# A decoder layer in split fp32: cross-attention queries made for four batches at a time, P.V for four heads, self-attention queries turned one step earlier

## The reference, cut to what matters

```python
hidden_states = jnp.concatenate([context, latents], axis=1)      # 256 keys a batch
q = (latents @ Wq).reshape(b, q_len, 4, 8, 128)                  # 4 groups of 8 heads
k = (hidden_states @ Wk).reshape(b, kv_len, 4, 128)
v = (hidden_states @ Wv).reshape(b, kv_len, 4, 128)
scores = jnp.einsum('bqhgd,bkhd->bhgqk', q, k) * scale
attn = jax.nn.softmax(scores, axis=-1)
out = jnp.einsum('bhgqk,bkhd->bqhgd', attn, v).reshape(b, q_len, 32 * 128)
x = x + out @ Wo
```

## Time and profile before

| what | value |
|---|---|
| runs | 1053.47 us median of 3 (1052.87 to 1053.89) |
| profiled execution | 1053.37 us, its span 1051.7 us |
| PE matmul | 1027.2 us busy (98%), 6808 matmuls |
| PE weight load | 916.8 us (87%) |
| VectorE, ScalarE, GpSimd | 645.4 (61%), 544.2 (52%), 385.5 us (37%) |
| TensorE's granted clock | 0.998 on average |
| data moved by DMA | 68.5 MB, 65 GB/s |
| self-attention, four groups, feed-forward (starts) | about 39, 317 and 917 us |

### The profile page before, as it was taken

How to read it: one execution, slowest core, us unless ns; L and a number is a source line. 1 busy time by engine, 2 the same in 40 slices (tenths; PEclk the granted TensorE clock), 3 DMA queues, 4 the chain that set the end, 5 groups by cost and what they waited for, 6 DMA issues and landing times.

```text
span 1051.7 us, 18418 instructions
## 1 busy us (share of the span) xinstructions
PE 1027.2 (98%) x6808; PEld 916.8 (87%) x6808; DVE 645.4 (61%) x1369; ACT 544.2 (52%) x1657; POOL 385.5 (37%) x370
## 2 busy tenths in 40 slices
PE   6999999999999999999999999999999999999997
PEld 5677777777889999999999999999999999799996
DVE  6788888887436555546545556555555575556554
ACT  5666666666526555536445446455545456522111
POOL 3544544544235324316224325225234236511110
PEclk9999999999999999999999999999999999999999
DMA  8300111105652003112022111121211013200000
GB/s 327 115 28 21 34 41 42 41 21 141 175 162 82 25 31 112 61 41 61 21 79 63 63 45 55 50 61 51 81 51 51 31 61 122 74 7 20 20 21 21
DMA packets 70114, 68.53 MB, mean 65 GB/s; under 512 B 3984, under 2 KB 53904, under 8 KB 70032
## 3 DMA queue, kind: packets, MB, share of 16 engines
q1 hardware_dynamic: 70032, 67.43, 20.5%
HBM read 48.55 MB, written 18.87 MB: 64 GB/s over the span
## 4 chain that ended last, share of the span: by engine, by line
PE 92%; DVE 4%; ACT 2%; issue 1%; DMA 1%; SPq 0%; POOLq 0%; POOL 0%; DVEq 0%; ACTq 0%
PE bank L218 27%; PE bank L220 26%; PE bank L219 26%; PE bank L945 5%; PE bank L729 2%; PE bank L689 1%; PE bank L693 1%; PE bank L699 1%; ACT Pb L1192 1%; DVE b_nb L1545 1%; PE bank L696 1%; DVE b_max L1542 1%; PE bank L611 1%; DMA rawKV<-in_L_attn_Wv_dram 1%; DVE PTal L1304 0%
## 5 line engine op out<-in xcount | busy, mean ns | idle before, releaser
L548 POOL TENSOR_TENSOR Pb<-Pb,b_rec 128x512 f32<-128x512 f32 x128 | 133.1, 1040 | 353.1 <-DVE b_rec L1549 352.7
L218 PE MATMUL bank<-XTh,WQh 128*128 128x256 f32 x512 | 145.9, 285 | 2.5 <-DVE Ql L1304 2.4
L220 PE MATMUL bank<-XTh,WQl 128*128 128x256 f32 x512 | 144.9, 283 | 0.0
L219 PE MATMUL bank<-XTl,WQh 128*128 128x256 f32 x512 | 144.8, 283 | 0.0
L1192 ACT ACTIVATE Pb<-bank,b_nb 128x256 f32<-128x256 f32 x256 | 119.0, 470 | 40.8 <-DVE b_nb L1545 40.1
L1304 DVE TENSOR_TENSOR Ol<-bank,Oh 128x256 fp32r<-128x256 f32 x128 | 54.0, 422 | 116.0 <-ACT Oh L1055 113.8
L1055 ACT ACTIVATE PTh<-bank 128x512 fp32r<-128x512 f32 x128 | 76.7, 599 | 85.3 <-PE bank L945 85.1
L1110 ACT ACTIVATE Pa<-bank,a_nb 128x128 f32<-128x128 f32 x256 | 90.4, 367 | 44.8 <-DVE a_nb L1425 44.8
L218 PE MATMUL bank<-WOh,Oh 128*128 128x512 f32 x256 | 110.0, 430 | 1.2 <-DVE x_res L1559 1.2
L510 POOL TENSOR_TENSOR Pa<-Pa,a_rec 128x512 f32<-128x512 f32 x64 | 68.2, 1066 | 104.6 <-DVE a_rec L1431 104.0
L218 PEld LDWEIGHTS bank<-XTh,WQh 128*128 128x128 f32 x512 | 97.7, 191 | 8.8 <-DVE Ql L1304 4.1
(11 more groups left out here) (230 smaller groups left out, 2865.0 us busy)
## 6 DMA issues: line engine op xcount, KB each, us to landing
kv_scratch<-KVst SPq DMA_DIRECT2D x64, 256.0 KB, 3.1
KV<-kv_scratch SPq DMA_DIRECT2D x32, 512.0 KB, 3.5
raw<-in_L_xattn_Wo_dram SPq DMA_DIRECT2D x32, 256.0 KB, 3.3
raw<-in_L_xattn_Wq_dram SPq DMA_DIRECT2D x24, 256.0 KB, 4.3
cx<-in_ctx_dram SPq DMA_DIRECT2D x8, 256.0 KB, 9.2
raw_first<-in_L_xattn_Wq_dram SPq DMA_DIRECT2D x8, 256.0 KB, 4.8
raw<-in_L_ffn_up_w_dram SPq DMA_DIRECT2D x8, 256.0 KB, 3.6
raw<-in_L_ffn_down_w_dram SPq DMA_DIRECT2D x8, 256.0 KB, 2.6
```

The costliest lines, as they stand in the source:

```text
L218: pe.matmul(dst, lh, rh, start=start, stop=False)
L219: pe.matmul(dst, lh, rl, start=False, stop=False)
L220: return pe.matmul(dst, ll, rh, start=False, stop=stop)
L548: gp.tensor_tensor(pk, pk, b_rec[:, k % 4, :].unsqueeze(2).to_broadcast([P, 2, KEYS]), ALU.mult).then_inc(b_g_norm, 1)
```

## The change

Queries are made for four batches at once, with 512 columns (`XTh[:, kc, cols]` of half the batches), in two steps a head: `kcs` (0, 1) in the even and (2, 3) in the odd step. Steps 0 to 15 of a group make batches 4 to 7, steps 16 to 31 batches 0 to 3 of the next group (none in the last). `Qh` and `Ql` keep their size and hold one half of the batches; the cells are laid out so that head pair i of one half overwrites batch i of the other, which has been scored. All eight heads of batches 0 to 3 of group 0 are made ahead of the loop, the last one in step 0.

P.V is made for four heads (two steps) at once: 512 columns, in even steps right after the scores and ahead of the transposes, for the two steps before. `PTh` and `PTl` hold the two steps side by side. Oh and Ol are evicted once for two steps with 512 columns, at that place on their engines: on ScalarE ahead of PTh, on VectorE after the maximum and ahead of PTl.

The next group's query weights are split in steps 8, 10, to 22. In the last group the up chunks are split in steps 6, 8, to 20, the down chunks in steps 17, 19, 21 and 27 to 31.

In the self-attention the rotated queries of batch b+1 are turned in step 6, and ScalarE and VectorE split them in that step; the keys stay in step 7.

```diff
-                steps += [(17 + h, "wq", h) for h in range(XG)]
+                steps += [(8 + 2 * h, "wq", h) for h in range(XG)]
             else:
-                steps += [(17 + i, "ffn", i) for i in range(NUP)]
+                steps += [(6 + 2 * i, "ffn", i) for i in range(NUP)]
                 steps += [(22 + i - NUP, "ffn", i) for i in range(NUP, NUP + NFC)]
-                steps += [(min(26 + i - NUP - NFC, DUOS), "ffn", i) for i in range(NUP + NFC, NF)]
+                steps += [(26, "ffn", NUP + NFC)]
+                steps += [((17, 19, 21, 27, 28, 29, 30, 31)[c], "ffn", NUP + NFC + 1 + c) for c in range(IC)]
+        QBANK = (2, 3, 5, 4, 6, 7, 6, 7)
+        HALF = NB // 2
+        def query_cells(t, head, half):
+            i, h = head // 2, head % 2
+            return t[:, :, h, i, :] if half else t[:, i, h, :, :]
...
+            def queries(g_count, head, half, bk, kcs=range(KC)):
                 pe.wait_ge(b_g_w, g_count)
+                cols = slice(half * HALF * P, (half + 1) * HALF * P)
+                for kc in kcs:
+                    op = split3(pe, bank[bk][:], WQh[:, head, kc, :], WQl[:, head, kc, :],
+                                XTh[:, kc, cols], XTl[:, kc, cols], kc == 0, kc == KC - 1)
...
+                    if j == 6 and not last:
+                        turn_q(b + 1)
                     if j == 7 and not last:
-                        turn_qk(b + 1)
+                        turn_k(b + 1)
...
-            first_queries((6, 7))
-            pe.wait_ge(v_ul, U_E0 + 1)
+            pe.wait_ge(v_ul, NU)
+            first_queries(4)
             scores_b(0, 1)
+            first_queries(5)
+            pe.wait_ge(b_v_q, 5)
+            first_queries(6)
+            def outputs(g, q):
+                pe.wait_ge(b_v_pt, DUOS * g + 2 * q + 4)
+                pe.wait_ge(b_v_o, QUADS * g + q + 1)
+                slot = (q // QB) % 3
                 for c in range(2):
...
+                    op = split3(pe, bank[5][:], vh, vl, PTh[:, c, :], PTl[:, c, :], c == 0, c == 1)
...
+                    if k and k % 2 == 0:
+                        outputs(g, k // 2 - 1)
                     pe.wait_ge(b_g_norm, DUOS * g + k + 1)
...
+                    if k < BLOCK or not last:
+                        head, kcs = (k % BLOCK) // 2, ((0, 1), (2, 3))[k % 2]
                         if k % 2 == 0:
+                            pe.wait_ge(b_v_q, XG + 2 * XG * g + k // 2 - (1 if g == 0 and k == 0 else 0))
+                        if k < BLOCK:
+                            queries(W0 + WPG * g, head, 1, 6, kcs)
                         else:
+                            queries(W0 + WPG * g + XG + head + 1, head, 0, 6, kcs)
-                    if k:
-                        outputs(g, k - 1)
                 out_piece(g, NB - 1, 0)
+                outputs(g, QUADS - 1)
```

On ScalarE (VectorE in the same manner, with `lo`):

```diff
                 for k in range(DUOS):
+                    if k and k % 2 == 0:
+                        outputs(g, k // 2 - 1)
                     act.wait_ge(b_pe_pt, DUOS * g + k + 1)
-                    hi(PTh[:, k % 2, :], bank[3 + k % 2][:]).then_inc(b_a_pt, 1)
+                    hi(PTh[:, :, (k % 2) * KEYS:(k % 2 + 1) * KEYS],
+                       bank[3 + k % 2][:].rearrange("p (c n) -> p c n", c=2)).then_inc(b_a_pt, 1)
...
                     split_weights(k)
-                    if k:
-                        outputs(g, k - 1)
-                outputs(g, DUOS - 1)
+                outputs(g, QUADS - 1)
...
+                    if j == 6 and not last:
+                        q_hi(b + 1)
                 if not last:
-                    qk_hi(b + 1)
+                    k_hi(b + 1)
```

More of the change, by code:

```diff
@@ L52 @@
 PB = XG // 2
+QUADS = DUOS // 2
+BLOCK = NB // 2 * PB
+QB = PB // 2
 INT, LAT, NE = 1024, 256, 8
@@ L311, in decoder_layer, with ffn_ready, query_cell @@
         CBANK = (6, 7, 2, 3, 5, 0, 1, 6)
-        QBANK = (2, 3, 5, 4)
+        def ffn_ready(i):
+            order = [n for n, (_, kind, j) in enumerate(chunk_steps(True)) if kind == "ffn" and j == i]
+            return W0 + WPG * (XKV - 1) + order[0] + 1
+        QBANK = (2, 3, 5, 4, 6, 7, 6, 7)
[3 more added lines that the diff above has]
+            return t[:, :, h, i, :] if half else t[:, i, h, :, :]
+        def query_cell(t, head, b):
+            i, h = head // 2, head % 2
+            return t[:, b % HALF, h, i, :] if b // HALF else t[:, i, h, b % HALF, :]
         LN3_STEPS = (14, 16)
@@ L699, in scores, with first_queries @@
                     pe.matmul(bk[:], QTh[rows, m, :], Kbdl[rows, m, :], start=False, stop=True).then_inc(pe_s, 1)
-            def queries(g_count, head, pair, bk):
+            def queries(g_count, head, half, bk, kcs=range(KC)):
                 pe.wait_ge(b_g_w, g_count)
[L705 to L714, removed]
+                cols = slice(half * HALF * P, (half + 1) * HALF * P)
+                for kc in kcs:
+                    op = split3(pe, bank[bk][:], WQh[:, head, kc, :], WQl[:, head, kc, :],
+                                XTh[:, kc, cols], XTl[:, kc, cols], kc == 0, kc == KC - 1)
+                if KC - 1 in kcs:
+                    op.then_inc(b_pe_q, 1)
+            def first_queries(h):
+                queries(h + 1, h, 0, QBANK[h])
             def batch(b, last):
@@ L1195, in probs_b, with queries @@
                 op.then_inc(b_a_exp, 1)
-            def queries(count, fill, parity, bk=6):
-                act.wait_ge(b_pe_q, 2 * count)
-                hi(Qh[:, parity, 2 * fill:2 * fill + 2, :],
-                   bank[bk][:].rearrange("p (h n) -> p h n", h=2)).then_inc(b_a_q, 1)
+            def queries(n, head, half, bk=6):
+                act.wait_ge(b_pe_q, n + 1)
+                hi(query_cells(Qh, head, half), bank[bk][:].rearrange("p (b n) -> p b n", b=HALF)).then_inc(b_a_q, 1)
             for n in range(4):
@@ L1208, in _ @@
             act.wait_ge(pe_u, NU)
-            queries(1, 0, 0, QBANK[0])
-            queries(2, 1, 0, QBANK[1])
-            queries(3, 2, 0, QBANK[2])
+            for h in range(4):
+                queries(h, h, 0, QBANK[h])
             probs_b(0, 0)
-            queries(4, 3, 0, QBANK[3])
+            queries(4, 4, 0, QBANK[4])
             probs_b(0, 1)
+            queries(5, 5, 0, QBANK[5])
+            queries(6, 6, 0, QBANK[6])
             act.wait_ge(b_g_w, W0)
@@ L1549, in reciprocals, with queries @@
                 dve.reciprocal(b_rec[:, k % 4, :], b_sum[:, k % 4, :]).then_inc(b_v_rec, 1)
-            def queries(count, fill, parity, bk=6):
-                dve.wait_ge(b_a_q, count)
-                lo(Ql[:, parity, 2 * fill:2 * fill + 2, :], bank[bk][:].rearrange("p (h n) -> p h n", h=2),
-                   Qh[:, parity, 2 * fill:2 * fill + 2, :]).then_inc(b_v_q, 1)
+            def queries(n, head, half, bk=6):
+                dve.wait_ge(b_a_q, n + 1)
+                lo(query_cells(Ql, head, half), bank[bk][:].rearrange("p (b n) -> p b n", b=HALF),
+                   query_cells(Qh, head, half)).then_inc(b_v_q, 1)
             def residual(g, b):
@@ L1609, in group @@
                         maxima_b(gg, kk)
+                    if k and k % 2 == 0:
+                        outputs(g, k // 2 - 1)
+                    if g == 0 and k == 0:
+                        queries(7, 7, 0, QBANK[7])
                     dve.wait_ge(b_a_pt, DUOS * g + k + 1)
-                    lo(PTl[:, k % 2, :], bank[3 + k % 2][:], PTh[:, k % 2, :]).then_inc(b_v_pt, 1)
+                    cols = slice((k % 2) * KEYS, (k % 2 + 1) * KEYS)
+                    lo(PTl[:, :, cols], bank[3 + k % 2][:].rearrange("p (c n) -> p c n", c=2),
+                       PTh[:, :, cols]).then_inc(b_v_pt, 1)
                     if ahead:
@@ L1615, in group @@
                         residual(g, k // PB - 1)
-                    if k % 2 == 1 and (k < DUOS - XG or not last):
-                        queries(4 + 16 * g + k // 2 + 1, (k % XG) // 2, (k // XG + 1) % 2)
-                    if k:
-                        outputs(g, k - 1)
+                    if k % 2 == 1 and (k < BLOCK or not last):
+                        queries(XG + 2 * XG * g + k // 2, (k % BLOCK) // 2, k < BLOCK)
                     if last:
```

121 lines of the change are left out of this document (62 added, 59 removed).

## The result

The changed kernel takes 1037.44 us (median of 4 runs, 1036.92 to 1039.74), the kernel before 1053.43 beside it (4 runs, 1052.87 to 1053.89). The ratio is 0.9853 with a 95% interval of 0.9836 to 0.9870: 16.0 us less. The forecast was 1038.5 in a range of 1030 to 1047.

A forecast was written before the change was run, and what follows sets the result against it. The prediction took PE to bound the kernel. Its terms, -11.5 - 2.0 - 0.5 + 1.2 - 2.2 = -15.0 us, led from 1053.5 to 1038.5, range 1030 to 1047.

The forecast's parts named there:

- (1): Cross-attention queries: 1536 narrow matmuls become 768 wide ones at 0.230 us; -11.5 us together with P.V.
- (2): Cross-attention P.V: 768 narrow matmuls become 384 wide ones at 0.230 us; -11.5 us together with the queries.
- (3): Group starts: wait for Ql nearly covered, a smaller one for PTl in its place; -2.0 us (0 to -3.9).
- (4): Last group, steps without queries: 2.6 of 3.1 us of waiting left, PE should bind; -0.5 us (+4 to -2.5).
- (5): Group ends: output piece 2 waits 0.4 us for Oh and Ol in three groups; +1.2 us (0 to 2).
- (6): Self-attention step 6: turned queries fill PE's wait for PTal, 0.32 us a batch; -2.2 us (0 to -3.7).
- Rival A: Wide matmuls cost 0.2375 us wherever other engines are busy: widths give 2.9 instead of 11.5, so 1047; chance 0.10.
- the small issue gap: Skill's isolated matmul gap, N/2.4 + 2.5 ns: the 1152 saved issues would be worth 2.9 us, not 11.5.
- The ring between ScalarE and VectorE: Last group's steps without queries, before: maximum, exponential, weight, Oh, Ol, maximum take 3.64 us; forecast broken at odd steps.
- rival B: ScalarE-VectorE ring stays in all 16 light steps of the last group: 7.0 us of waiting, so 1043; chance 0.10.
- Rival D: Self-attention: turning queries early does nothing, PTal stays the limit; 1040.7; chance counted with the forecast's, 0.66 together.
- Rival C: Every quad's P.V waits for PTl or delays the exponential behind it; slower, 1060.9 at 0.35 us each; chance 0.04.

The follow-up runs named there:

- e5: Changed kernel with queries and P.V both narrow (256 columns) and the rotated queries turned in step 7, leaving the order of work; 1050.32 us.
- e1: Changed kernel with the turn and split of the rotated queries put back to step 7; 1040.11 us.
- e2: Kernel before the change with only the turn and split of the rotated queries moved to step 6; 1049.35 us.
- e10: Changed kernel with the places of XT and WO in SBUF exchanged, nothing else; 1036.76 us.
- e7: Changed kernel with P.V behind the transposes in step 2 of each group and in the last group's even steps from 18; 1033.27 us.
- e8: Changed kernel with the next group's first scores put between output pieces 1 and 2 (counted from 0) of a group's last batch; 1034.88 us.
- e3: Changed kernel with P.V for four heads made by twelve matmuls of 256 columns instead of six of 512; 1039.84 us.
- e4: Changed kernel with queries made by twelve matmuls of 256 columns in each step instead of six of 512; 1045.76 us.
- e6: Changed kernel with GpSimd's low parts of the two weight chunks of step 0 made in step 1 of each group; 1035.47 us.
- e9: Changed kernel with the changes of e6, e7 and e8 all together; 1031.49 us.

## Why the prediction was right, point by point

| step | forecast | measured | from |
|---|---|---|---|
| (1), (2) widths | -11.5 | -12.3 | e5, before and after, without waits; -10.2 by the medians of e5 and e1 |
| (3) group starts | -2.0 | -2.4 | waits of 3.9 before, 1.5 after |
| (4) last group | -0.5 | +0.3 | waits of 3.5 before, 3.8 after |
| (5) group ends | +1.2 | +1.0 | 3 x 0.32 |
| (6) turn | -2.2 | -3.0 | e1, e2 |
| sum | -15.0 | -16.4 | -16.5 by the two stretches (13.5 and 3.0), -16.0 by the medians |

(1) and (2): the right mechanism, and the size chosen (0.230) lay between the two kinds: queries are at 0.227, P.V at 0.232. Undone one at a time, a pair of queries was worth 11.3 ns in a group's period and one of P.V 6.1, where the forecast gave both 10. That the two add up to so near the forecast is in part luck: it had one price for both and none for the scores behind the queries. Rival A (0.2375) is refuted; so is the small issue gap, which had led to nearly the same time.

(3) was right in kind and nearly in size: the wait for Ql went, PTl came in its place, at the same spot, with b_nb held for the same reason. P.V was forecast 0.3 to 0.4 late and is 0.42 with the slow distance behind it.

(4) did not bring its 0.5, within its bounds. Whether it cost anything is not shown: with the same order in the last group its waits are 3.8 us in the change, 3.4 in e10 and 4.3 in e1, and 3.5 before. The ring between ScalarE and VectorE did break (rival B, 7.0 of waiting, did not come). The forecast counted five or six waits for PTl and 1 us for the statistics; five came, one of them through the statistics, but the residual's wait, 1.22 before, stayed at 1.04, and the forecast names no such wait in what it leaves. e7 shows what the step was worth had P.V not stood ahead of the transposes: 2.2 us.

(5) was right: 0.32 for 0.4.

(6) was too small. The forecast let 0.2 of the 0.44 through in step 7, and 0.25 came through; it took 0.12 for the small waits of the next batch's scores, and those gave 0.17. Both sizes were too small, the mechanism was right: the period fell by 0.42 for the forecast 0.32. Rival D, that the turn does nothing, is refuted.

Rival C would have had PE wait for PTl in normal steps. None does: apart from the last group, all waits for it lie in step 2 of a group.

The time, 1.1 us below the forecast, is nearer than the terms are: (1), (2), (3) and (6) gave 0.4 to 0.8 us more than forecast, (4) about 0.8 less.

## What to carry to other kernels

Where one engine is busy all the time, the cost of its instructions is the distance between their starts, and doubling the width of a matmul pays what two distances have over one: here 11 to 12 ns a pair of queries and 6 to 7 ns a pair of P.V, 12 us in 1152 pairs. Fusing the products of two steps leaves less time between the making of the later operand and its use. In the middle of a group other work fills that time, at its edges such work is missing; look there for the new wait, and fill it with independent work (the next scores) before moving the product itself, which brought the old wait back. A tiny VectorE instruction that takes as long as a GpSimd one beside it is a sign to move the GpSimd one, which cost nothing here.

## What the runs showed of the hardware

**A short drop of the clock makes 1.4 to 1.6 us of an execution.** In all twelve traces PE has a hole of 1.6 us right ahead of the first transposes of the self-attention. In some profiled executions the granted clock falls behind it from its upper level (2.4 GHz) to its lower (1.2 GHz, shown as 0.50), in e1 in the stretches from 41 to 44 us; in others it does not. The table by stretch, first e1_turn_back, then before:

```profile
41.00:42.00 1.00, 0.99 (x2) 0.83 (x3) 1.00 (x3) 0.17 (x1) 0.00 (x0) 0.50 0.00 0
42.00:43.00 1.00, 1.00 (x4) 0.77 (x3) 1.00 (x3) 0.36 (x2) 0.00 (x0) 0.50 0.00 0
```

```profile
41.00:42.00 1.00, 0.63 (x4) 0.42 (x4) 1.00 (x2) 0.93 (x3) 0.02 (x1) 1.00 0.85 254
42.00:43.00 1.00, 0.76 (x3) 0.66 (x4) 1.00 (x3) 0.40 (x1) 0.00 (x0) 1.00 0.02 9
```

From the first transposes of the self-attention to the second ones it is then 7.27 us instead of 5.85 (e1; 7.34 in e5, 7.36 in e8, 7.44 to 7.46 in e3, e4 and e6). Before, after, e2, e7, e9 and e10 do not show the drop. What decides it is not shown. The first transposes themselves lie between 39.37 and 42.09 us from the start of the span, and five of the six executions with a drop are the five with the earliest (39.4 to 40.5), so that the two differences often cancel. Together these make differences of up to 4 us between executions that the change has nothing to do with: the profiled execution of e5 took 1054.75, its other five runs 1049.5 to 1050.5. Terms below 2 us have to be read from periods in the traces, not from spans.

**The distance of wide matmuls depends on more than the width.** The medians are 0.227 (queries), 0.229 to 0.234 (output pieces) and 0.232 (P.V) in one kernel. In e2, with the same places and shapes as before, the 384 narrow query distances of a group add up to 45.95 us instead of 46.17, most of the 0.30 by which its groups are shorter. It is not the address of the moving operand (e10); no run here isolates what it is. So a difference of 0.3 us a group between two kernels can come without any cause in the change.

**The distance is not a fixed price plus the columns.** In the changed kernel's groups the transposes (128 columns) follow each other after 0.109, the narrow matmuls (256) after 0.120 and the wide queries (512) after 0.227: 11 ns more for the first doubling, 107 for the second. What sets the distance of the narrow ones is open; each has a weight load of its own, whose records last 0.191 in the kernel before, and no run here takes it away.

**A small VectorE instruction is held until GpSimd's ends.** A b_nb usually takes 0.17 us. In all twelve traces each one of over 0.25 us (25 before, 34 in the change) ended 0.02 to 0.03 us after the end of a GpSimd instruction that it had overlapped. Where both start together, some ns decide. With GpSimd's weight chunk 0 to 9 ns ahead b_nb was held in every trace (858.47, 865.40 and 878.78 in the change), with the chunk 3 ns or more behind it took 0.17 (867.48, 874.00 and 887.06 in e3). At 1 or 2 ns behind it went either way: 0.17 at 860.95 in e3, 1.32 at 875.34 in e5.

**The first distance behind a wait or behind transposes is longer**: 0.31 to 0.34 for 512 columns where 0.23 is usual (490.22 to 490.54 in the changed kernel), and 0.20 to 0.22 instead of 0.12 for 256. Behind transposes this costs next to nothing: the matmul itself starts 0.028 after the last transpose (490.19 to 490.22), where transposes are 0.109 apart. Behind a wait it is a loss: e6 gained the whole 0.42 (0.31 of waiting and 0.11 in the first distance).
